# Attention and routed-expert block on one core: ten surplus-block tiles run first, expert pipeline one step deeper, unread products in TensorE's waits

## What is computed

```python
x = x + tanh(g_xattn) * attention(layernorm(x), ctx, W, b)
xf = layernorm(x).reshape(-1, 256)
logits = xf @ expert_sel.T
sel_val, sel_idx = top_k(sigmoid(logits), 4)
gates = zeros((N, 64)).at[arange(N)[:, None], sel_idx].set(sel_val)
h = einsum('nd,kde->nke', xf, keys)            # keys 64 x 256 x 128
out = einsum('nke,kev->nv', relu(h) * gates[:, :, None], values)   # values 64 x 128 x 256
x = x + tanh(g_ffn) * out
```

## Time and profile before

| | |
|---|---|
| runs of the kernel | 323.28, 323.54, 323.6 us |
| profiled execution: span from first to last instruction | 268.6 us (it is the only time given for it; 54.9 us of the median lie around the span) |
| PE / PE weight loads / DVE / ACT / POOL busy | 209.1 / 170.5 / 146.9 / 117.0 / 144.1 us |
| chain that ended last, by engine | PE 45%, DMA 15%, DVE 12%, issue 8%, POOL 6%, SP's queue 6%, ACT 6% |
| routing stage, until PE has the last rank | 0 to 100.5 us |
| wait for the last scatters and the first rows | 100.5 to 120.5 us |
| expert stage on PE | 120.5 to 231.4 us |
| last y scatter starts; first read of y is issued | 232.6; 236.5 us |
| combine stage | 236.5 to 268.6 us |
| moved by DMA | 67.5 MB, mean 251 GB/s |

### The profile page before, as it was taken

One profiled execution on the slowest core, in us unless ns is written; L12 is line 12 of the kernel. 1 busy time (PEld: TensorE's weight loads), 2 busy tenths in 40 slices (PEclk: granted clock), 3 DMA queues, 4 the chain that ended last, 5 costly groups with the idle time before them and its releaser, 6 DMA issues.

```text
span 268.6 us, 5359 instructions
## 1 busy us (share of the span) xinstructions
PE 209.1 (78%) x1290; PEld 170.5 (63%) x1291; DVE 146.9 (55%) x617; ACT 117.0 (44%) x383; POOL 144.1 (54%) x162
## 2 busy tenths in 40 slices
PE   6877896977966632709999988999999999409852
PEld 6654665655644421507989867899999999308741
DVE  3357368895788877002455534544545445166656
ACT  2355387866867630002555554544444444100110
POOL 4003254777777777711577777777777676400000
PEclk9796599997999555775999999999999999955996
DMA  5999999999999432236999999857655643169993
GB/s 150 260 277 313 357 334 324 361 362 361 359 318 342 135 110 98 98 76 182 318 369 375 366 289 375 249 157 222 189 174 147 175 116 109 44 225 405 379 416 140
DMA packets 47440, 67.49 MB, mean 251 GB/s; under 512 B 5909, under 2 KB 32683, under 8 KB 47408
## 3 DMA queue, kind: packets, MB, share of 16 engines
q1 hardware_dynamic: 38828, 48.12, 57.2%
q0 software_dynamic: 6912, 16.83, 17.4%
q10 hardware_dynamic: 1668, 2.17, 2.2%
HBM read 39.76 MB, written 29.43 MB: 258 GB/s over the span
## 4 chain that ended last, share of the span: by engine, by line
PE 45%; DMA 15%; DVE 12%; issue 8%; POOL 6%; SPq 6%; ACT 6%; DVEq 1%; ACTq 0%; POOLq 0%
PE bank L685 14%; DMA keys_sb<-y_rows 8%; PE bank L696 8%; POOL x_slots L472 6%; PE bank L673 6%; PE bank L703 5%; PE bank L513 4%; DMA rows<-x_slots 3%; SPq L362 3%; DVE xs L1239 2%; DMA shared<-in_L_xattn_W 2%; PE bank L605 2%; DVE xs L1021 1%; SPq L350 1%; PE bank L609 1%
## 5 line engine op out<-in xcount | busy, mean ns | idle before, releaser
L480 POOL DMA_INDIRECT y_rows<-rows,result_at x80 | 78.5, 981 | 39.9 <-ACT rows L917 15.5
L472 POOL DMA_INDIRECT x_slots<-rows,pos_i x64 | 63.0, 984 | 48.7 <-DVE pos_i L1004 26.0
L685 PE MATMUL bank<-xT,shared 128*128 128x128 f32 (+1 forms) x392 | 57.6, 278 | 0.5 <-ACT xT L912 0.5
L917 ACT COPY rows<-bank 128x256 f32<-128x256 f32 x80 | 29.9, 373 | 52.3 <-PE bank L696 35.9
L685 PEld LDWEIGHTS bank<-xT,shared 128*128 128x128 f32 x392 | 51.5, 196 | 0.9 <-ACT xT L912 0.9
L912 ACT COPY xT<-bank 128x256 f32<-128x256 f32 x82 | 30.9, 377 | 27.7 <-PE bank L673 27.4
L673 PE MATMUL bank<-ident,rows 128*128 128x128 f32 x164 | 32.8, 283 | 9.9 <-DMA rows<-x_slots 9.8
L696 PE MATMUL bank<-values_sb,shared 128*128 128x256 f32 x128 | 40.2, 396 | 0.0
L1162 DVE TENSOR_SCALAR shared<-bank 128x128 f32<-128x128 f32 x64 | 18.6, 291 | 38.4 <-PE bank L685 37.4
L673 PEld LDWEIGHTS bank<-ident,rows 128*128 128x128 f32 x164 | 23.2, 146 | 20.5 <-DMA rows<-x_slots 12.6
L618 PE MATMUL bank<-values_sb,probsT 120*128 120x320 f32 x32 | 14.7, 546 | 9.3 <-ACT probsT L879 9.2
(11 more groups left out here) (147 smaller groups left out, 320.3 us busy)
## 6 DMA issues: line engine op xcount, KB each, us to landing
x_slots<-values_sb SPq DMA_DIRECT2D x4, 2056.0 KB, 27.1
rows<-x_slots SPq DMA_DIRECT2D x64, 128.5 KB
keys_sb<-y_rows SPq DMA_DIRECT2D x16, 512.0 KB, 5.7
values_sb<-in_L_ffn_values SPq DMA_DIRECT2D x5, 1024.0 KB, 12.6
keys_sb<-in_L_ffn_keys SPq DMA_DIRECT2D x6, 512.0 KB
values_sb<-in_L_ffn_values SPq DMA_DIRECT2D x12, 256.0 KB
rows<-x_slots SPq DMA_DIRECT2D x42, 64.2 KB
xs<-in_x SPq DMA_DIRECT2D x8, 256.0 KB, 8.5
```

The lines of the kernel that those rows point to most:

```text
L472: pool.indirect_dma_start(x_slots, bass.IndirectOffsetOnAxis(ap=pos_i[:, t * K + k:t * K + k + 1].bitcast(U32), axis=0), rows[:, t % RB * ...
L480: pool.indirect_dma_start(y_rows, bass.IndirectOffsetOnAxis(ap=result_at[:, t:t + 1], axis=0), y_sb[:, t % R, :], None, bounds_check=last_ ...
L685: mm = pe.matmul(pH(t.mod(2))[:, a * width:(a + 1) * width], keys_now[:, t.mod(2), a, c * F:(c + 1) * F], xgT[:, t.mod(2), at:at + width], ...
L917: act.copy(y_sb[:, t.mod(R), :], pY(t.mod(2))).then_inc(e_y, 1)
```

## The change

- Tile order: first 10 tiles *o*, each two blocks of 64 rows, only blocks of experts 0 to 39 that lie wholly in the rows of the first `SEEN` = 13 routing tiles; then 40 e tiles; then three turns "eebeeeebee" (24 e, 6 b). 80 tiles and 16 pairs of blocks as before, more pairs in the loop behind. If there are fewer early blocks than 20, the places left are filled with expert 0's padding.
- SP starts the loads of the o tiles after the scatters of 13 tiles, and those of the e tiles after all 16. The o tiles have buffers of their own for rows and results, in the memory of the late weights. Those come between the loads of tiles 20 to 46.
- Tables: VectorE takes a snapshot of the ranks at tile 13, makes the table of early blocks first, and does the tables for the rest between its steps of tiles 0 to 8. PE's matmuls for them stand behind tiles 1 and 4.
- Pipeline: transpose 4 tiles ahead of the result (before 2), keys copy 3, hidden 2 (before 1); five buffers for `xgT` and for the hidden tile. e tiles multiply straight from `keys_sb`, so their 64 key copies on VectorE are gone.
- `unread` products: 4 behind the last attention tile, 2 + 2 + 6 around the table matmuls (before: 8 ahead of the stage).
- The run-time loop behind the 80 tiles is skipped as a whole when nothing is left.

The diff, cut:

```diff
-    ALONE = 4
-    MIXED = "eebebeebeb"
-    BOTH = 4
+    SEEN = 13
+    KINDS = "o" * R + "e" * (4 * R) + "eebeeeebee" * 3
+    HEAD = len(KINDS) // R
+    PAIRS = R + KINDS.count("b")
+    RING = 5
+    AHEAD_T, AHEAD_K, AHEAD_H = 4, 3, 2
...
         def rest_turns(eng, turn, used):
-            with eng.Fori(0, REST // 2) as i:
+            with eng.If(used > 0):
+                with eng.Fori(0, REST // 2) as i:
...
+            def turn_early(i):
+                at_rows = rows_at(early_rows[0:1, 2 * V * i:2 * V * (i + 1)], 2 * V)
+                for u in range(V):
+                    load_blocks(At(i * V + u), at_rows[2 * u], at_rows[2 * u + 1])
...
             def late_weights(n):
+                    if first + 4 > E - LATER and first <= E - LATER:
+                        sp.wait_ge(early_out, 16 * R)
...
-            sp.wait_ge(r_first, 1)
             sp.wait_ge(padded, 16 * E // FE)
-            sp.wait_ge(a_S, T)
-            sp.wait_ge(a_O, T)
-            for n in range(RB):
-                sp.wait_ge(scattered[n], 16 * K * len(range(n, T, RB)))
-            turn_alone(At(0), At(0))
...
+            scattered_to(SEEN)
+            sp.wait_ge(r_early, 1)
+            turn_early(0)
+            turn_early(1)
+            sp.wait_ge(r_first, 1)
+            scattered_to(T)
+            for i in range(1, 5):
+                turn_head(i)
             sp.wait_ge(r_table, 1)
+            for i in range(5, HEAD):
+                turn_head(i)
...
+            pool.memset(hidT_pair[:], 0.0).then_inc(hid_ok, 1)
...
+                if s == T + 1:
+                    pe.wait_ge(c_Mc, len(units))
+                    pe.wait_ge(weights_in, 16 * 2 * (E - LATE) // 8)
+                    unread(4)
             pe.wait_ge(p_picked, T)
             choices(T - 1, from_).then_inc(r_count, 1)
+            unread(2)
...
             pe.matmul(end_ps, upto[0:E, 0:E], units_bf[:], start=True, stop=True).then_inc(r_end, 1)
+            unread(2)
             pe.wait_ge(r_unit, 1)
+            pe.matmul(lead_ps[:, 0:2 * R], lead[:], unit_of[:, 0:2 * R], start=True, stop=True).then_inc(r_block, 1)
+            pe.matmul(expert_ps[:, 0:2 * R], expert_col[:], unit_of[:, 0:2 * R], start=True, stop=True).then_inc(r_block, 1)
+            unread(6)
...
+            def turn_head(i):
+                kinds = KINDS[i * V:(i + 1) * V]
+                pairs = V - kinds.count("e")
+                paired = block_experts(pe, At(pairs_before(i * V)), pairs) if pairs else []
+                for u, kind in enumerate(kinds):
+                    t = At(i * V + u)
+                    if t.offset:
+                        slots_T(t + AHEAD_T)
...
+                    if t.offset:
+                        hidden(t + AHEAD_H)
                     if kind == "e":
+                        result(t, expert_of_tile(t.offset))
                     else:
+                        result_pair(t, paired[u - kinds[:u].count("e")])
...
+                    if t.offset == 1:
+                        units_end()
+                    if t.offset == 4:
+                        units_block()
...
             def picks(t):
                 dve.wait_ge(p_R, t + 1)
+                if t == SEEN:
+                    dve.tensor_tensor(seen[:, 0:E - LATE], rank_ps[0:1, 0:E - LATE], base_row[:, 0:E - LATE],
+                                      ALU.subtract).then_inc(p_seen, 1)
...
+                    relu(t + AHEAD_H)
+                    keep_places(t + AHEAD_T)
+                    if t.offset == 0:
+                        count_units()
+                    if t.offset == 3:
+                        place_units()
+                    if t.offset == 6:
+                        unit_tables()
+                    if t.offset == 7:
+                        rest_counts()
+                    if t.offset == 8:
+                        raw_gates()
```

More of the change, by code:

```diff
@@ L566, in _, with unread @@
                 pe.matmul(bank[:, 6, 0:P], ident[:], ident[:], start=True, stop=True)
+            def unread(count):
+                for n in range(count):
+                    pe.matmul(pY(1), ident[:], values_sb[:, 0, :], start=True, stop=True)
             context_T(0)
@@ L678, in hidden @@
                 after(pe, e_Tc, t + 1)
-                after(pe, e_keys, t + 1)
                 after(pe, e_h, t - 1)
-                width = H if paired else P
-                for a in range(P // width):
+                kind = kind_of(t)
+                if kind == "e":
+                    expert = expert_of_tile(t.offset)
+                    weights = [keys_sb[:, expert * C:(expert + 1) * C, :].rearrange("p c f -> p (c f)")]
+                else:
+                    pair = pair_at(t)
+                    after(pe, e_keys, pair + 1)
+                    weights = [keys_now[:, pair.mod(2), a, :] for a in range(2)]
@@ L1214, in _, with turn_head @@
-            turn_mixed(At((HEAD - 1) * R), At(E - U), At(PAIRS - (R - U)), "bb")
+                dve.tensor_copy(keys_now[:, pair.mod(2), 0, :], keys_of(first)).then_inc(e_pair, 1)
+                dve.tensor_copy(keys_now[:, pair.mod(2), 1, :], keys_of(second)).then_inc(e_keys, 1)
+            later = KINDS + "b" * AHEAD_K
+            def turn_head(i):
+                ahead_of = later[i * V + AHEAD_K:(i + 1) * V + AHEAD_K]
+                pairs = V - ahead_of.count("e")
+                paired = block_experts(dve, At(AHEAD_K + i * V - later[:AHEAD_K + i * V].count("e")), pairs) if pairs else []
+                for u in range(V):
+                    t = At(i * V + u)
+                    if ahead_of[u] != "e":
+                        keys_pair(t + AHEAD_K, paired[u - ahead_of[:u].count("e")])
+                    relu(t + AHEAD_H)
+                    keep_places(t + AHEAD_T)
+                    if t.offset == 0:
+                        count_units()
[7 more added lines that the diff above has]
+                        raw_gates()
@@ L1215, in _ @@
+            waited = False
+            for i in range(2 * HEAD):
+                if "b" in later[i * V + AHEAD_K:(i + 1) * V + AHEAD_K] and not waited:
+                    waited = True
+                    dve.wait_ge(r_table, TABLE)
+                    dve.wait_ge(late_in, 16 * 3 * LATE // 4)
+                turn_head(i)
             used = rest_used(dve)
             def turn(t, pair):
-                paired = block_experts(dve, pair + 2, V)
+                paired = block_experts(dve, pair + AHEAD_K, V)
```

402 lines of the change are left out of this document (210 added, 192 removed).

## The result

The change did not make the kernel faster: 324.69 us (median of 20 runs) against 323.81 (20 runs) for the kernel before on the same chip, and a ratio of 1.0116, 95% interval 1.0083 to 1.0149. The forecast was 315.1, with 310.5 to 319.5 as its range. So the loss is 0.3% by the medians and 1.2% by the ratio: a gain like the forecast one is excluded, the size of the loss is not settled.

The account below looks back on a forecast made before the run. POOL's scatters, 1.285 us apart from tile 10, were to set the expert stage's end: reads at 228.1 instead of 236.5, -8.4, combine unchanged at 32.1, so span 260.2 and 315.1 us. Range 310.5 to 319.5, chance 0.73.

Parts of the forecast that it names:

- The ground it stood on: Starting profile: span 268.6 us, median 323.54; the difference was taken to lie outside the span and left unchanged.
- rival three: Early stage, o tiles 0 to 9 all at the lower clock: 1.9 us more per tile, 333.7 us; chance 0.05.
- Start of the early rows: From table chain to first rows: first o tile landed at 108.8 us, 11.7 earlier than before.
- The early stage and the clock: PE on the ten o tiles: full clock from the first, result 9 ends at 135.5 us, bounds 132.0 and 139.
- rival four: Slow start only: lower clock for 7 us, two tiles, or waits adding up to as much: +3.6, 318.7 us; chance 0.12.
- Unread products: Around the table: PE at work from about 95.5 to 108 us for the full clock; table end 105.2, not 104.4, if obstructive.
- POOL's end: From tile 10 on POOL never catches up: 69 intervals of 1.285 us, last scatter starts at 225.9, not 232.58.
- Rival two: Expert stage: POOL's interval falls to PE's pace because the copies go, PE sets the end: -15.9, 307.6 us; chance 0.06.
- The tail: Behind the last scatter: empty loop skipped, y lands 2.1 us later, reads begin at 228.1, combine keeps its 32.1.
- The sum: Whole kernel: reads at 228.1 instead of 236.5, -8.4 us, a span of 260.2 and a time of 315.1 us.

Follow-up runs that it names:

- the memsets: Three chained memsets on POOL ahead of each of five scatters, added to the changed kernel: 269.66 us against 265.12 on a quick chip; 1.0126 on a long one.
- after_3: The changed kernel with SP's wait for the y scatters against a constant, on a second quick chip: 265.12 us against 268.83 for the kernel before, 0.9870.

## Why the prediction was wrong

*The ground it stood on.* "Its own total is not given, so I put the difference on the median" is the step that failed first. A span of 268.6 against runs of 323.5 left 55 us unexplained, and every run since has 1.7 to 2.3 outside its span. The gap said that profile and times were not of one state of the machine; no rival of the five covered it. What the runs showed in its place: on long chips TensorE's results reach their readers late in the routing, table and expert stages, the gain of 11.7 us at the first transpose is 3.5 there and is gone by the first scatter of y (+2.6), and by tile 10 the changed kernel is 7.4 behind. Why those chips halt stays open. (A slip without weight: ten tiles at 1.88 us more each make 333.9 for rival three, not 333.7.)

*Start of the early rows.* 108.8 forecast, 108.4 on a quick chip: right. On long chips 134.6 to 136.6, which is 1.5 to 3.5 ahead of the kernel before instead of 11.7: POOL's lag behind the ranks, the source of this gain, is shorter there (8.8 to 10.2 us, not 14), and the table takes 6.1 instead of 3.3.

*The early stage and the clock.* "I take the full clock from the first o tile" was wrong: 0.53 over 107 to 115. Tile 10's scatter came 0.6 to 2.3 us late (137.8 and 139.5 for 137.2), less than rival four's 3.6; that the clock is the whole reason is argued, not shown. The rule that I had weighed, that waits for DMA bring back the lower clock (the Trainium skill, "TensorE: Matmul & The Clock Gate", "HAM oscillation"), describes this better than my step did: a wait of 3.19 us for rows, then 0.50 from 108 to 116.

*Unread products.* Costed at nothing, with 0.8 us more for the table as the bound, and taken for the reason of a higher clock. They give nothing on quick chips. On the one long chip with both, the kernel with 14 of them is 1.6% above the one without by the ratios and 0.6% by the medians: as much as the whole measured loss. By which wait they cost it was not found.

*POOL's end.* Interval 1.285 forecast, 1.281 measured, with no gap on a quick chip, and the memsets show that it is the bound. Rival two fell: the key copies of the e tiles are gone and the interval is unchanged. The trace shows no sign here of the rule of the Trainium skill, "SBUF — State Buffer", "Who interferes with whom"; whether these copies, 0.31 us each before, were of the fast kind that it speaks of no row tells. On long chips POOL idles 50 us, and the step does not apply.

*The tail.* Combine 32.1 measured and forecast. The wait for the gates is gone, as forecast, but the last scatter took 2.9 to land in after_3, not 2.1, so the reads come 3.1 behind it.

*The sum.* On quick chips -3.3 and -3.7 us by the medians, where -8.4 was forecast. The mechanism is right there, the size is not. Two executions with profiles were 0.8 and 2.9 us over the forecast span, and the profile that the forecast started from, 268.6, is itself 1.4 to 1.7 above the span that goes with the medians of the kernel before (269.11 and 268.83, less 1.9), which a single profile could not tell. Nor does one run tell 0.2%: on long chips the kernel before spreads over 4%. There, where the number was given, it is +0.9 us at the medians: the gain ahead of tile 10 is not there, and POOL, which was to set the end, waits for results.

## What to carry to other kernels

Compare the span of a profile with the times before using either. Here 1.7 to 2.3 us lay between them in every run; where it was 55, profile and times were not of one state, and a gain worked out on one has to be argued again for the other. A gain made of one engine's lag behind another is only as large as that lag: 13 to 14 us on quick chips, 5 to 10 in the profiles of long ones. Products that only keep the clock up have to be measured both with and without; these kept it up over a stretch without work and had lost it when the work came. And where runs spread over 4%, a term of 1 us has to be looked for in the profile, since the times do not show it.

## What the runs showed of the hardware

The same program takes 269 us on two chips and 318 to 324 on three others. On the latter, products of TensorE are seen by their readers up to 5 us late, again and again, in long parts of the expert stage every 7 to 8.5 us. In the case looked at closely the lag is 2.5 and 3.2 us, with the granted clock at 1.00 until the halt was over; it also comes when TensorE has nothing behind the product (3.7 us). POOL's scatters (1.28 us apart when results wait for them) and the combine stage (32 to 33 us on both) go at their usual pace. Leaving out half of the hidden products does not make the halts fewer in proportion; with 28 products that nobody reads the ratio is 1.0151, with none 0.9936 to 0.9982. What halts TensorE's results was not found: it could be a property of the chips, or something else that runs on them, and no kernel of one core here could tell these apart.
